# Attention of a two-layer kernel: score banks handled in two halves instead of whole

## What is computed

```python
def _L1_attn_ref(x, w_qkv, w_o):
    B, T, D, H = (2, 256, 256, 16)
    DH = D // H
    b, t, d = x.shape
    qkv = (x @ w_qkv).reshape(b, t, 3, H, DH)
    q, k, v = (qkv[:, :, 0], qkv[:, :, 1], qkv[:, :, 2])
    scale = 1.0 / np.sqrt(DH).astype(np.float32)
    scores = jnp.einsum('bqhd,bkhd->bhqk', q, k) * scale
    causal = jnp.tril(jnp.ones((t, t), dtype=bool))
    scores = jnp.where(causal[None, None], scores, -jnp.inf)
    attn = jax.nn.softmax(scores, axis=-1)
    out = jnp.einsum('bhqk,bkhd->bqhd', attn, v).reshape(b, t, d)
    return out @ w_o
...
x = x + _L1_attn_ref(xn, ...) + _L1_ffn_ref(xn, ...)
```

## Time and profile before

| | us |
|---|---|
| median of 3 runs (lowest, highest) | 1609.53 (1601.91, 1615.94) |
| the profiled execution | 1612.19 |
| its span, first to last instruction | 1610.5 |
| PE busy in the span | 1431.0 |
| mean granted TensorE clock, share of full | 0.958 |

### The profile page before, as it was taken

One profiled execution on the slowest core, in us unless ns is written; L12 is line 12 of the kernel. 1 busy time (PEld: TensorE's weight loads), 2 busy tenths in 40 slices (PEclk: granted clock), 3 DMA queues, 4 the chain that ended last, 5 costly groups with the idle time before them and its releaser, 6 DMA issues.

```text
span 1610.5 us, 28864 instructions
## 1 busy us (share of the span) xinstructions
PE 1431.0 (89%) x10753; PEld 1164.4 (72%) x10753; DVE 826.8 (51%) x2179; ACT 501.7 (31%) x971; POOL 555.7 (35%) x634
## 2 busy tenths in 40 slices
PE   7996999999999998999997888888888859998865
PEld 6885789999999996666655666656665537786754
DVE  4554444444444444788875566566556514333324
ACT  2221122222222223333332444434443324433310
POOL 2444321111111112222224345544543354456451
PEclk9998999999999998999998899999999969999987
DMA  5893811111111115000002010101100003434432
GB/s 175 147 108 47 92 47 52 47 47 51 49 47 51 50 44 154 1 0 0 0 13 60 21 37 25 37 25 34 28 25 11 2 14 117 127 122 141 121 110 77
DMA packets 73181, 94.73 MB, mean 59 GB/s; under 512 B 14877, under 2 KB 61367, under 8 KB 73056
## 3 DMA queue, kind: packets, MB, share of 16 engines
q1 hardware_dynamic: 55440, 56.54, 15.4%
q0 software_dynamic: 17616, 36.48, 8.1%
HBM read 60.66 MB, written 32.31 MB: 58 GB/s over the span
## 4 chain that ended last, share of the span: by engine, by line
PE 77%; DVE 10%; issue 5%; ACT 3%; DMA 3%; another core or an unknown queue 1%; POOL 0%; DVEq 0%; SPq 0%; ACTq 0%; POOLq 0%
PE score L1561 47%; PE mixed L1561 17%; PE side L1561 9%; DVE WGU L1438 5%; ACT ARENA L941 2%; PE side L1763 2%; DMA xn_rows<-XN 2%; DMA X<-in_u 1%; PE side L1828 1%; PE side L1570 1%; PE side L1709 0%; PE side L1899 0%; DVE w_in L1068 0%; DVE ARENA L1457 0%
## 5 line engine op out<-in xcount | busy, mean ns | idle before, releaser
L706 POOL DMA_INDIRECT XN<-xn_rows,slot_tok x149 | 141.8, 952 | 408.6 <-PE side L1763 374.6
L1561 PE MATMUL score<-xT,HT 128*128 128x128 f32 x1136 | 208.0, 275 | 0.0
L1438 DVE TENSOR_REDUCE WGU<-score 128x4 f32<-128x512 f32 (+1 forms) x128 | 116.6, 953 | 149.4 <-PE score L1561 149.4
L1561 PE MATMUL score<-ARENA 32*128 32x256 f32 (+1 forms) x2048 | 123.0, 355 | 54.4 <-DVE WGU L1438 38.9
L1561 PEld LDWEIGHTS score<-xT,HT 128*128 128x128 f32 x1136 | 166.8, 192 | 0.0
L1561 PEld LDWEIGHTS score<-ARENA 32*128 32x128 f32 x2048 | 83.0, 189 | 91.6 <-DVE WGU L1438 57.2
L1239 DVE TENSOR_TENSOR HT<-sh_gu,score 128x128 f32<-128x128 f32 (+1 forms) x149 | 71.2, 478 | 145.7 <-ACT sh_gu L907 69.9
L656 POOL DMA_INDIRECT lists<-token_no,w_in x128 | 127.2, 993 | 48.2 <-issue 40.6
L742 POOL TENSOR_SCALAR_AFFINE_SELECT ARENA<-ARENA 128x512 f32<-128x512 f32 x128 | 78.3, 634 | 164.1 <-ACT ARENA L941 163.8
L1561 PE MATMUL mixed<-ARENA,HT 128*128 x568 | 134.2, 379 | 0.0
L941 ACT ACTIVATE ARENA<-score 128x1536 f32<-128x1536 f32 x64 | 92.9, 1452 | 125.4 <-PE score L1561 125.4
(11 more groups left out here) (249 smaller groups left out, 2667.5 us busy)
## 6 DMA issues: line engine op xcount, KB each, us to landing
y_rows<-sh_gu SPq DMA_DIRECT2D x149, 128.0 KB
xn_rows<-XN SPq DMA_DIRECT2D x32, 256.0 KB
WGU<-in_gu SPq DMA_DIRECT2D x8, 1024.0 KB
X<-in_u SPq DMA_DIRECT2D x16, 256.0 KB
ARENA<-in_dn SPq DMA_DIRECT2D x8, 512.0 KB
out<-X SPq DMA_DIRECT2D x16, 256.0 KB
XN<-xn_rows,slot_tok POOLq DMA_INDIRECT x149
lists<-token_no,w_in POOLq DMA_INDIRECT x128
```

What stands on the lines that cost most here:

```text
L706: x["got"][j % RING].mark(eng.indirect_dma_start(XG[j % RING], None, xn_rows[l], bass.IndirectOffsetOnAxis(slot_tok[:, j:j + 1], 0)))
L1438: ins = eng.tensor_reduce(o, score[:, :, c * P:(2 * c + 1) * P], AX.X, ALU.max, negate=True)
L1561: return eng.matmul(o, l, r, start=start, stop=stop)
```

## The change

`scores` and `scores_t` become one function `scores(h, s, t)`. It works on a half h of the banks: for group `s` it makes scores (and two masks) in banks 2h and 2h + 1, and beside them, in turns with it, the transposed scores of another group `t` in the other two banks. A turn has eight such half steps. Each event of the banks (`s`, `max`, `t`, `exp`, `sel`) is now a pair, one per half. `maxima`, `exps` and `causal` work on two banks each, so they are called eight times a turn instead of four. The transposed scores come one half step to two steps later than before, so that half of group 1 and all of groups 2 and 3 fall in the next turn, where the sequence is `d`, and its `weigh` of group 0 moves there too.

`queries`, `keys` and `values` are split in two parts with a wait each, and ACT's copies of queries and keys likewise (256 columns instead of 512). DVE adds layer 0's results in two pieces, takes statistics before the output is added, runs `maxima(b, 2, 1)` ahead of the logits' copy, and splits `pick_experts` in two. POOL's scatters and gathers are spread differently over the steps, and `list_tokens` of turn 17 over six steps instead of two.

```diff
-        def causal(r, i):
-            A["exp"].wait(eng, r.n * GROUPS + i)
+        def causal(r, i, h):
+            A["exp"][h].wait(eng, r.n * GROUPS + i)
             unfuse(eng)
             for t in range(CH):
-                m = PT[i % 2][:, :, 2 * t, :]
+                m = PT[i % 2][:, 2 * h:2 * h + 2, 2 * t, :]
...
-            for step, (r, i) in enumerate(((d, 2), (d, 3), (b, 0), (b, 1))):
+            for step, (r, i, h) in enumerate(((d, 1, 1), (d, 2, 0), (d, 2, 1), (d, 3, 0), (d, 3, 1), (b, 0, 0), (b, 0, 1), (b, 1, 0))):
...
-        def exps(r, i):
+        def exps(r, i, h):
             n = r.n * GROUPS + i
-            A["t"].wait(eng, n)
+            A["t"][h].wait(eng, n)
             A["pv"].wait(eng, n, 2)
-            A["exp"].mark(act(PT[i % 2].rearrange("p r b q -> p r (b q)"), score[:, :, 0:HALVES * P], ACT.Exp))
+            A["exp"][h].mark(act(PT[i % 2][:, 2 * h:2 * h + 2, :, :].rearrange("p r b q -> p r (b q)"),
+                                 score[:, 2 * h:2 * h + 2, 0:HALVES * P], ACT.Exp))
...
-        def maxima(r, i):
-            A["s"].wait(eng, r.n * GROUPS + i)
+        def maxima(r, i, h):
+            A["s"][h].wait(eng, r.n * GROUPS + i)
             j, e = i // 2, i % 2
             for c in range(CH):
-                o = NM[:, c, j, :].rearrange("p (r z) -> p r z", z=ROWS)[:, :, DH * (1 - e)]
-                ins = eng.tensor_reduce(o, score[:, :, c * P:(2 * c + 1) * P], AX.X, ALU.max, negate=True)
-            A["max"].mark(ins)
+                o = NM[:, c, j, :].rearrange("p (r z) -> p r z", z=ROWS)[:, 2 * h:2 * h + 2, DH * (1 - e)]
+                ins = eng.tensor_reduce(o, score[:, 2 * h:2 * h + 2, c * P:(2 * c + 1) * P], AX.X, ALU.max, negate=True)
+            A["max"][h].mark(ins)
...
+        def scores(h, s, t):
+
+
+            if s:
+                r, i = s
+                A["exp"][h].wait(eng, r.n * GROUPS + i, 3)
+                if r.n == 0 and 0 < i < 3:
+                    A["max"][h].wait(eng, i - 1)
+                if h == 0 and i % 2 == 0:
+                    A["qc"].wait(eng, 2 * r.n + i // 2)
+                    A["kc"].wait(eng, 2 * r.n + i // 2)
+            if t:
+                r, i = t
+                n = r.n * GROUPS + i
+                A["qp"].wait(eng, 2 * r.n + i // 2)
+                if n + 2 < NSEQ * GROUPS:
+                    A["max"][1 - h].wait(eng, n + 2)
+                else:
+                    A["exp"][1 - h].wait(eng, n - 1)
+            for part in range(CH):
+                if s:
+                    r, i = s
+                    c = part
+                    for q in (2 * h, 2 * h + 1):
+                        band = slice(ROWS * q, ROWS * (q + 1))
+                        mm(score[:, q, c * P:(2 * c + 1) * P], QM[r.u][band, i % 2, i // 2, c * P:(c + 1) * P],
+                           KM[r.u][band, i % 2, i // 2, 0:(c + 1) * P], c == 0, False)
+                if t:
+                    r, i = t
+                    c = 1 - part
+                    for q in (2 - 2 * h, 3 - 2 * h):
+                        band = slice(ROWS * q, ROWS * (q + 1))
+                        ins = mm(score[:, q, 2 * c * P:(2 + c) * P], KM[r.u][band, i % 2, i // 2, c * P:(c + 1) * P],
+                                 QM[r.u][band, i % 2, i // 2, c * P:SEQ], True, True)
+            if t:
+                A["t"][1 - h].mark(ins)
+            if s:
+                for q in (2 * h, 2 * h + 1):
+                    ins = mm(score[:, q, :].rearrange("p (a k) -> p a k", a=2)[:, :, 0:P], ident_b[:, :],
+                             future_b[:, :].unsqueeze(1).broadcast_to([P, CH, P]), False, True)
+                A["s"][h].mark(ins)
```

More of the change, by code:

```diff
@@ L1474, in attention @@
             if b:
-                maxima(b, 1)
+                maxima(b, 1, 0)
+            if c:
+                combine(c, [1])
+            if b:
+                maxima(b, 1, 1)
+            if b and not a:
+                table_index(2)
+            if c:
+                stats_stage(c)
             if o:
                 add_out(o)
-            if c:
-                stats_stage(c)
             if b:
+                maxima(b, 2, 0)
                 shift(b, 0)
+                maxima(b, 2, 1)
             if a:
@@ L1495, in attention @@
             if b:
-                maxima(b, 3)
-            if b and not a:
-                table_index(2)
+                maxima(b, 3, 1)
             if d:
@@ L1837, in project_out @@
             A["wo"].mark(ins)
[L1839 to L1851, removed]
-                for k in range(KD):
-                    ins = mm(bank[4][:, m * SEQ:(m + 1) * SEQ], w_qkv[:, k, m * P:(m + 1) * P], xT[r.u][:, k, :], k == 0, k == KD - 1)
-            A["q"].mark(ins)
@@ new lines, in queries @@
+        def queries(r, m):
+            if m == 0:
+                N[1]["lgc"].wait(eng, r.n)
+                if r.v == 0 and not is_first(r):
+                    RT[1]["rkc"].wait(eng, r.i - 1)
+                if r.n == 13:
+                    eng.wait_ge(s_slots, 2)
+            else:
+                A["qc"].wait(eng, 2 * r.n)
+            for k in range(KD):
+                ins = mm(bank[4][:, m * SEQ:(m + 1) * SEQ], w_qkv[:, k, m * P:(m + 1) * P], xT[r.u][:, k, :], k == 0, k == KD - 1)
+            A["q"].mark(ins)
@@ L1887, in weigh @@
         def weigh(r, i):
-            A["sel"].wait(eng, r.n * GROUPS + i)
+            for h in range(2):
+                A["sel"][h].wait(eng, r.n * GROUPS + i)
             at = i % 2 * SEQ
@@ L1896, in turn_maxima @@
         def turn_maxima(r, j):
-            A["max"].wait(eng, r.n * GROUPS + 2 * j + 1)
+            for h in range(2):
+                A["max"][h].wait(eng, r.n * GROUPS + 2 * j + 1)
             for c in range(CH):
@@ L1958, in attention @@
                 logits_stage(1, a)
-            if b:
-                if not d:
-                    at_max(1)
-                scores(b, 2)
+            scores(1, now(2), now(0))
             if a:
-                queries(a)
-            if b:
-                at_max(2)
-                scores_t(b, 0)
+                queries(a, 0)
+                keys(a, 0)
+            scores(0, now(3), now(0))
             if d:
@@ L1970, in attention @@
             if a:
-                keys(a)
-            if b:
-                scores(b, 3)
+                queries(a, 1)
+            scores(1, now(3), now(1))
             if d:
                 turn_mixed(d)
-            if b:
-                at_max(3)
-                scores_t(b, 1)
-                A["vc"].wait(eng, b.n)
-                A["on"].wait(eng, b.n, 1)
-                weigh(b, 0)
-                if a:
-                    A["kc"].wait(eng, a.n)
-                turn_maxima(b, 1)
+            if a:
+                keys(a, 1)
         eng.wait_ge(s_l1a, 48)
```

193 lines of the change are left out of this document (102 added, 91 removed).

## The result

| | before | after |
|---|---|---|
| median (lowest, highest), us | 1612.74 (1601.91, 1617.53) | 1593.14 (1587.31, 1598.11) |
| ratio, 95% interval | | 0.9881 [0.9835, 0.9927] |
| profiled execution, its span | 1612.19, 1610.5 | 1595.26, 1593.5 |
| granted TensorE clock | 0.958 | 0.954 |

A forecast was written before the change was run, and what follows sets the result against it. PE's work was taken as interlocked with the banks' hand-overs between PE, DVE and ACT, 27.6 us a turn. 1612.2 - 27 (13 turns) - 6 (turn 17) - 9 (tail) = 1570 us, 1567 against the median; range 1545 to 1596.

The forecast's parts named there:

- PE's work in a turn: Attention stage, second layer: PE's own work summed over all steps of one turn, 23.2 us, nothing removed by the change.
- rival (2): Scores and transposed scores do not run beside each other: 32.3 us a turn, 1663 us in all; chance 0.05.
- Maxima and exponentials of a half: DVE's maxima of a half step taken as 1.0 us, ACT's exponentials of 768 columns as 0.81 us.
- Rival (1): Halves cost as much as wholes, maxima 1.82 us: 27.6 us a turn, 1601 us; chance 0.12 with mixtures.
- The three waits: PE's new waits per turn: logits' copy 1.6, second pair's shift 0.25, turning of maxima 0.3; sum 2.15 us.
- the first wait: Next sequence's queries wait for the logits' copy behind DVE's maxima: 1.4 us, 0.36 more with token places, 1.6 on average.
- rival (3): PE's clock falls in every turn, costing 2 to 3 us: 28 us a turn, about 1602 us; chance 0.03.
- a granted clock under 0.9 between turns 4 and 16: Sign named beforehand that the forecast is wrong and that rival (3) holds.
- PE busy above 90%: Sign named beforehand that the forecast is right, together with ends of turns 25 to 25.5 us apart.
- The table in turn 9: Turn with the first half's table, where PE stood still 4.53 us: about 3 us kept, making 332 for 13 turns.
- Turn 17: Turn without a new sequence, 28.8 us before: 18 us of PE work, eight hand-overs 19, forecast 22.5, -6.
- The tail: The attention stage's last stretch, 35.2 us before: forecast 26 us, -9.

The follow-up runs named there:

- the kernel with the weighing last: Changed kernel with PE making the logits ahead of `weigh(d, 2)` instead of behind it: 1518.24 us, one execution.
- the second profile: The changed kernel run once more, unaltered, on the first chip: 1595.98 us, ratio 0.9842 to the kernel before.

## Why the prediction was wrong

The hand-overs were hidden as forecast, and a turn at full clock has nearly the forecast length. What failed in the 13 turns is one step: a wait was costed as its own length, with no price for the clock behind it.

**PE's work in a turn**: forecast 23.2 us. From one turn's first half step to the next are 27.13 us (1125.67 to 1152.80); less the pause in front of the queries (1.42, counted from where they would have started), 0.46 in front of the turning of the maxima (the same way) and 1.75 of slow clock, 23.5. Passes are 0.94 us for 16 as before, so rival (2) is out. The 0.3 too little are small things: groups of queries or keys split in fours take 0.96 to 1.07 us from start to start, not 0.91, and two masks hand over to a weighing after 0.31 us, not 0.22.

**Maxima and exponentials of a half**: groups of instructions by form, 800 to 1400 us, beside the earlier trace rows:

```profile
L1458 DVE TENSOR_REDUCE WGU<-score 128x2 f32<-128x512 f32 x128 | 87.3, 682 | 0.0
L1458 DVE TENSOR_REDUCE WGU<-score 128x2 f32<-128x256 f32 x128 | 54.3, 424 | 153.3 <-PE score L1591 151.2 <-issue 1.8 <-DVE tile_expert L1160 0.2
L944 ACT ACTIVATE ARENA<-score 128x768 f32<-128x768 f32 x128 | 103.8, 811 | 148.3 <-PE score L1591 145.9 <-issue 2.0
```

A pair of reduces takes 1.02 us in the time line above (forecast 1.0), an exponential 0.81 (0.81). Rival (1) is out. PE waits neither for ACT nor for POOL's selects in ordinary turns; costing the selects at nothing and ACT's extra work below PE's was right.

**The three waits**: right in kind and close in size. The logits' copy costs 1.2 to 1.6 us (forecast 1.4, or 1.76 with token places), the turning of the maxima waits 0.3 us in ten of the 13 turns (the output addition is named in four), the shift next to nothing but for 1.4 us once. Without the fall a turn is 25.2 or 25.8 us, where 25.3 stood.

**The failed step** is "1.6 on average" for the first wait, with the pause as its whole price. The clock falls behind it in 12 of 13 turns, and that is 12 x 1.8 = 22 us. Forecast for the turns with the table were 332 us; measured are 355.2, and 333.6 without the falls. This is rival (3), and it had a chance of 0.03. It was weighed on "0.99 over 359 us with 50 us of short idle times", as if pauses were alike. The new one was longer than most of those (30.1 us in 39 waits for the maxima, 0.8 each) and came a half step behind the logits, the thinnest matmuls of the turn; which of the two matters more is not shown. The rival's time, 1602 us, from 28 us a turn, was 9 us too long, nearer than the forecast's 1567; the weight was what failed. Its sign, a granted clock under 0.9 between turns 4 and 16, was set too low: 12 falls of 3.5 us left 0.94. And PE busy above 90%, named as a sign of being right, came true (93%) in part by slow work. The page "TensorE: Matmul & The Clock Gate" of the Trainium skill, section "A second HAM failure mode: psum-queue depth-cycling", cited there on clocks that swing with frequent small pauses between groups of matmuls, pointed the right way: the clock swings between 1.00 and 0.53 in a turn. But it swings at one pause a turn, where the many shorter ones of before went with 0.99, and the kernel with the weighing last shows 1.19 and 1.58 us of pause without it.

**The table in turn 9**: costed at 3 us, it cost nothing: turn 9 takes 27.5 us like its neighbours. It stands behind maxima that no longer hold PE up there. Where the pause is gone, 4.3 us of it return on the first chip and 2.5 on the third.

**Turn 17**: forecast 22.5 us, measured 28.5, the second error. PE's time line:

```profile
1278.07 0.44 PE L1953 MATMUL side<-ident,WGU 128*128 128x128 f32 x2 [1.97 <-DVE X L1483]
...
1279.83 1.66 PE L1591 MATMUL score<-ARENA 32*128 32x128 f32 x16 [0.53 <-issue]
```

The turning of the maxima waits for the output addition on DVE, which stands behind the second table, and the half step behind it runs at the low clock (0.50 from 1279.83 to 1284.80 us). But moving the table and keeping the clock at 1.00 brought turn 17 only from 28.6 to 27.0 us on the third chip. The larger part is PE's own work: I had put it at 18 us, where the earlier trace rows already had PE busy for 21.09, and at full clock it is 20.9 us in that kernel. With it no half step lasts only the 2.4 us of a hand-over: from 1262.13 us on they start 2.5 to 5.0 us apart.

**The tail**: forecast -9. From turn 17's mark to the end of the program are 303.6 us against 313.1: -9.5. The stretch of 35.2 us is now 26.1, where 26 were forecast. ACT's idle 8.93 us are now 2.40:

```profile
1302.41 0.60 ACT L957 ACTIVATE sh_gu<-mixed 128x512 f32<-128x512 f32 x1 [2.40 <-PE mixed L1591]
```

This hit is partly luck. In the profile of the kernel before on the third chip the same copy, at 1312.00, comes after 3.15 us of idle, not 8.93, and from turn 17's mark to the end the gain is 5.5 us (263.1 to 257.6). So the stall of 8.93 us is not a fixed part of the kernel before; what made it is not shown.

**Together**: of the 1612.2 us the start gave -3.1, the 13 turns -4.1 (forecast -27), turn 17 -0.4 (forecast -6), the tail -9.5 (forecast -9): 1595.1, and 1595.26 were measured. The start, up to turn 3, was not forecast. The range held the time by 3 us; the forecast's own number was 26 us off, 22 of them the clock in the 13 turns and 6 turn 17. The range's low end was not what its terms give: 24.3 a turn, 3 for the table and -12 behind make 1557 us, not 1545.

## What to carry to other kernels

A new wait on the engine that bounds a stage has two prices: its length, and what the engine's clock does behind it; look what work stands ahead of it, and give the second price a real chance (that thin work ahead raises it is a hint of one execution). A tiny operation that a large engine waits for, here a copy of 16 columns, belongs ahead of long ones in its queue: that order was worth more (2.0% and 2.4%) than the whole change (1.0% to 1.6%). To see such a loss, compare busy time at equal instruction counts: 10753 instructions before and after, 22.8 us more.

## What the runs showed of the hardware

- The clock's fall is not settled by program and pause: the two rows of one execution, 54 us apart, differ behind the same operations and the same pause. Slow turns come in runs (turns 6 to 14 in the second profile), and so do the others, so that turns of one execution are no independent trials. What the clock goes by stays open; these runs show only that useless matmuls in the pause (three or one), or a weighing instead of logits ahead of the half step, went with 13 of 13 turns at full clock, one profile each.
- Useless matmuls on the bounding engine made the kernel faster: 0.9741 of before against 0.9842 for the changed kernel on that chip, 337.3 against 352.1 us in the 13 turns.
- Chips differ by 3% in this kernel, 1612 against 1560 us for the profiled executions of before, and nearly all of it lies behind turn 17, most of that in the last stage, the experts. The 13 turns take 359.2 and 353.1 us; from turn 17's mark to the end are 313.1 and 263.1. The same stretch of the kernel before on the first chip and, below, on the third:

```profile
1400.00:1500.00 100.00, 90.19 (x537) 75.76 (x535) 37.68 (x103) 36.80 (x113) 55.67 (x59) 0.95 0.43 129
```

```profile
1400.00:1500.00 100.00, 97.19 (x601) 82.89 (x602) 44.87 (x121) 41.79 (x125) 64.06 (x67) 1.00 0.52 153
```

DMA moves 129 GB/s there against 153, and PE is idle for 9.8 against 2.8 us. Why the one chip is slower was not looked into; ratios were taken on one chip each for that reason.
